# Two GNN layers on one core: the bf16 split of Q and R moves from the node stage into the first layer's loop over edges

## What is computed

```
h   = relu(layernorm(x))
# layer 0, for every edge (src, dst) with its 64 attributes e
a   = relu([h[src], h[dst], e] @ We1 + be1)        # 320 -> 32
m   = relu(a @ We2 + be2)                          # 32 -> 128
b   = relu([h[dst], m] @ Wn1 + bn1)                # 256 -> 64
n   = relu(b @ Wn2 + bn2)                          # 64 -> 128
x   = x + h + segment_sum(n, dst)
# layer 1
h   = relu(layernorm(x))
msg = ((h @ W[etype])[src] + b[etype]) * weight
x   = x + relu(segment_sum(msg, dst))
```

## Time and profile before

| what | value |
|---|---|
| median of 3 runs | 8001.07 us (7994.84 to 8001.35) |
| the profiled execution, its own time | 7997.6 us |
| its span, first to last instruction | 7995.8 us |
| TensorE busy | 6820.1 us (85%) |
| POOL busy | 5906.7 us (74%) |
| VectorE busy | 4067.4 us (51%) |
| ScalarE busy | 2015.2 us (25%) |
| granted TensorE clock, mean | 0.933 |
| data moved by DMA | 572.29 MB, mean 72 GB/s |

### The profile page before, as it was taken

One profiled execution on the slowest core, in us unless ns is written; L12 is line 12 of the kernel. 1 busy time (PEld: TensorE's weight loads), 2 busy tenths in 40 slices (PEclk: granted clock), 3 DMA queues, 4 the chain that ended last, 5 costly groups with the idle time before them and its releaser, 6 DMA issues.

```text
span 7995.8 us, 199814 instructions
## 1 busy us (share of the span) xinstructions
PE 6820.1 (85%) x52954; PEld 5270.5 (66%) x52954; DVE 4067.4 (51%) x13463; ACT 2015.2 (25%) x4976; POOL 5906.7 (74%) x6251
## 2 busy tenths in 40 slices
PE   5999999999999999999978788888788778878887
PEld 4766666666666666667656666666666666666666
DVE  6444444444444444444455555555555555555555
ACT  5433333333333333333330000000000000000000
POOL 4777777777777777777757777777777777777776
PEclk7999999999999999999988988888888988898888
DMA  6333333333333333333332222222222222222222
GB/s 131 85 83 83 83 83 83 83 83 83 83 83 83 83 83 83 83 83 83 83 85 55 55 55 55 55 55 55 55 55 55 55 55 55 55 55 55 55 55 77
DMA packets 646407, 572.29 MB, mean 72 GB/s; under 512 B 325139, under 2 KB 520987, under 8 KB 645452
## 3 DMA queue, kind: packets, MB, share of 16 engines
q0 software_dynamic: 198624, 253.43, 15.0%
q1 hardware_dynamic: 447324, 313.26, 13.8%
HBM read 544.44 MB, written 21.68 MB: 71 GB/s over the span
## 4 chain that ended last, share of the span: by engine, by line
POOL 43%; issue 26%; PE 20%; DMA 7%; SPq 1%; DVE 1%; POOLq 1%; ACT 1%; DVEq 0%; ACTq 0%
POOL shared L589 30%; POOL rows_place L589 12%; PE bank L1165 12%; DMA rows_place<-h_tab,idx 6%; PE bank L1178 3%; PE bank L1167 2%; SPq L520 1%; ACT h_place L636 1%; PE bank L1180 1%; DMA h_place<-h_tab 0%; PE bank L1076 0%; POOLq L387 0%; POOLq L584 0%; PE bank L1095 0%; DMA qr_tab<-late 0%
## 5 line engine op out<-in xcount | busy, mean ns | idle before, releaser
L589 POOL DMA_INDIRECT shared<-p_tab,idx x3128 | 2956.6, 945 | 994.5 <-issue 957.4
L589 POOL DMA_INDIRECT rows_place<-h_tab,idx x3079 | 2906.4, 944 | 960.6 <-issue 865.6
L1165 PE MATMUL bank<-shared,rows_place 128*128 128x256 f32 x6158 | 1831.9, 449 | 642.5 <-DMA rows_place<-h_tab,idx 387.2
L1165 PEld LDWEIGHTS bank<-shared,rows_place 128*128 128x128 f32 x6158 | 1291.6, 220 | 909.4 <-DMA rows_place<-h_tab,idx 430.2
L982 DVE SCALAR_TENSOR_TENSOR shared<-bank,key,late 128x256 f32<-128x256 f32 x3128 | 1292.6, 476 | 839.7 <-PE bank L1167 687.3
L745 ACT ACTIVATE h_place<-bank 128x256 f32<-128x256 f32 x782 | 300.4, 384 | 3501.8 <-PE bank L1167 2956.8
L1076 PE MATMUL bank<-h_sb,w_tile 128*128 128x128 f32 x6256 | 907.7, 288 | 69.3 <-DVE h_sb L899 0.9
L1076 PEld LDWEIGHTS bank<-h_sb,w_tile 128*128 128x128 f32 x6256 | 758.5, 191 | 279.4 <-DVE h_sb L899 279.0
L899 DVE TENSOR_SCALAR h_sb<-bank,be_col 128x128 f32<-128x128 f32 x782 | 273.9, 350 | 1237.0 <-PE bank L1069 1237.0
L1095 PE MATMUL bank<-wn_half,h_sb 128*128 128x128 f32 x6256 | 890.0, 285 | 0.0
L1178 PE MATMUL bank<-h_place,w_rel_sb 128*128 128x64 f32 x6256 | 852.1, 294 | 0.0
(11 more groups left out here) (98 smaller groups left out, 5081.8 us busy)
## 6 DMA issues: line engine op xcount, KB each, us to landing
rows_place<-in_dst_c SPq DMA_DIRECT2D x782, 192.0 KB
h_place<-h_tab SPq DMA_DIRECT2D x6272, 0.5 KB
shared<-in_edge_cols SPq DMA_DIRECT2D x782, 128.0 KB
shared<-p_tab,idx POOLq DMA_INDIRECT x3128
rows_place<-h_tab,idx POOLq DMA_INDIRECT x3079
qr_w<-qr_tab SPq DMA_DIRECT2D x782, 18.0 KB
qr_tab<-late SPq DMA_DIRECT2D x21, 336.0 KB, 5.5
res<-in_x SPq DMA_DIRECT2D x14, 448.0 KB, 6.9
```

Of the source, the lines that this page charges most:

```text
L589: pool.indirect_dma_start(out=rows_of[s][:, t, :], out_offset=None, in_=table, in_offset=bass.IndirectOffsetOnAxis(ap=idx[k][:, s * TC + t ...
L1165: pe.matmul(bank[s][:, 0:RW], there, hot_rel[s % 2][:, t, :], start=(t == 0), stop=(t == TC - 1))
```

## The change

- The table of Q and R is one f32 table of 96 columns. It is stored group by group in the node stage beside P, from four small buffers `pqr` (two in `late`, two in `rows_place`), which no longer lie in `agg`. The split into parts is gone, and so is its wait. ScalarE copies `pqr` out of PSUM in place of VectorE, and waits before the fifth and each later group until the stores from that buffer have landed.
- In layer 0's loop SP loads the window of 32 f32 rows three times over, into 96 partitions (`qr_f`). For each chunk ScalarE copies 64 of these to PSUM and rounds all 96 to bf16 (`split_first`), VectorE subtracts (`remainder`), ScalarE rounds 64 partitions (`split_second`), and VectorE writes the last 32 (`last_part`). The split of a chunk is spread over the steps two and one ahead of its use (three for `split_first`).
- In the node stage VectorE normalises all 7 tiles (`scale_x`) and POOL takes the relu. Between the layers ScalarE normalises tiles 0 to 3 of a group and POOL tiles 4 to 6, then the relu of those.
- `agg` is cleared at the start, half by POOL and half by ScalarE. `dst_f` is converted in the node stage. The edge types are converted ahead of the work between the layers, not behind it.
- The source indices of the first two quads of chunks are both loaded ahead of the loop.

The core of the diff:

```diff
-    qr_tab = nc.dram_tensor("qr_tab", [3, NPAD, QR], bf16).ap()
+    qr_tab = nc.dram_tensor("qr_tab", [NPAD, QR], f32).ap()
...
+        pqr = [t[:, k * TPG * P:(k + 1) * TPG * P].rearrange("p (j d) -> p j d", d=P)
+               for t in (pqr_late, rows_place) for k in range(2)]
+        qr_f = [hT[0][0:3 * W, s * QR:(s + 1) * QR] for s in range(SL)]
+        ps_split = [bank[7][0:2 * W, s * QR:(s + 1) * QR] for s in range(SL)]
...
# sync, node stage
             for g in range(NG):
                 sp.wait_ge(pqr_copied, 2 * g + 2)
-                sp.dma_start(node_rows(p_tab, g), group(pqr, g)[:, :, 0:H1]).then_inc(p_stored, 16)
-                if g == RANGE_AT:
+                sp.dma_start(node_rows(p_tab, g), pqr[g % PQ][:, :, 0:H1]).then_inc(p_stored[g % PQ], 16)
+                sp.dma_start(node_rows(qr_tab, g), pqr[g % PQ][:, :, H1:P]).then_inc(p_stored[g % PQ], 16)
+                if g == RANGE_AT - 2:
                     sp.wait_ge(range_set, 3)
...
-            for q in range(NPART):
-                sp.wait_ge(lo_done, q + 1)
-                for t in range(3):
-                    sp.dma_start(node_rows(qr_tab[t], q * (PT // TPG), PT // TPG), qr_part[q % PB][t]).then_inc(parts_stored[q % PB], 16)
...
# sync, layer 0's loop
-                    sp.wait_ge(h2_summed[s], c.turn + 1)
+                    sp.wait_ge(split_hi[s], c.turn + 1)
                     hold(sp)
-                    sp.dma_start(qr_w[s][:, :], qr_tab[:, ds(start, W), :]).then_inc(qr_landed[s], 16)
+                    sp.dma_start(qr_f[s][:, :], qr_tab[ds(start, W), :].rearrange("(a w) o -> a w o", a=1).broadcast_to([3, W, QR]))\
+                      .then_inc(qr_landed[s], 16)
...
# gpsimd, node stage
+            pool.memset(agg[:, 0:NPAD // 2], 0.0).then_inc(agg_zeroed, 1)
             for g in range(NG):
-                pool.wait_ge(h_done, g + 1)
+                pool.wait_ge(xn_done, g + 1)
+                pool.tensor_scalar_max(h[g % HB], h[g % HB], 0.0).then_inc(relu_done, 1)
+                pool.wait_ge(relu_done, g + 1)
                 pool.tensor_tensor(group(res, g), h[g % HB], group(res, g), ALU.add).then_inc(res_done, 1)
...
# gpsimd, between the layers, behind the memset of a group
+                for j in range(t0, t1):
+                    at = g * TPG + j
+                    ins = pool.tensor_scalar(h[g % HB][:, j, :], res[:, at, :], mv[:, at, 0:1], rstd[:, at:at + 1],
+                                             ALU.subtract, ALU.mult)
+                ins.then_inc(h_high_scaled, 1)
+                pool.wait_ge(h_high_scaled, g + 1)
+                pool.tensor_scalar_max(h[g % HB][:, t0:t1, :], h[g % HB][:, t0:t1, :], 0.0).then_inc(h_high_done, 1)
...
# scalar, layer 0's loop
+            def split_first(c):
+                s = c.slot
+                act.wait_ge(qr_landed[s], 16 * c.turn + 16)
+                act.activation(ps_split[s], qr_f[s][0:2 * W, :], ACT.Copy)
+                act.activation(qr_w[s][:, :], qr_f[s][:, :], ACT.Copy).then_inc(split_hi[s], 1)
+
+            def split_second(c):
+                act.wait_ge(split_res, c.n + 1)
+                act.activation(qr_w[c.slot][0:2 * W, :], ps_split[c.slot], ACT.Copy).then_inc(split_mid, 1)
...
# vector, node stage
+            def scale_x(g):
+                if g >= HB:
+                    dve.wait_ge(h_transposed, 2 * (g - HB + 1))
+                    dve.wait_ge(res_done, g - HB + 1)
+                for j in range(TPG):
+                    at = g * TPG + j
+                    ins = dve.tensor_scalar(h[g % HB][:, j, :], res[:, at, :], mv[:, at, 0:1], rstd[:, at:at + 1],
+                                            ALU.subtract, ALU.mult)
+                ins.then_inc(xn_done, 1)
...
# vector, layer 0's loop
+            def remainder(c, before=None):
+                s = c.slot
+                dve.wait_ge(split_hi[s], c.turn + 2)
+                if before:
+                    last_part(before)
+                dve.tensor_tensor(ps_split[s], ps_split[s], qr_w[s][0:2 * W, :], ALU.subtract).then_inc(split_res, 1)
+
+            def last_part(c):
+                s = c.slot
+                dve.wait_ge(split_mid, c.n + 1)
+                dve.tensor_tensor(qr_w[s][0:W, :], ps_split[s][0:W, :], qr_w[s][0:W, :], ALU.subtract).then_inc(split_lo[s], 1)
...
# tensor, layer 0's loop
-                pe.wait_ge(qr_landed[s], 16 * c.turn + 16)
+                pe.wait_ge(split_lo[s], c.turn + 1)
```

More of the change, by code:

```diff
@@ L124, in gnn_two_layers @@
         range_row = late[0:1, QC * CH:QC * CH + NROW]
-        pqr = agg[:, :].rearrange("p (j d) -> p j d", d=P)
-        PT = 2 * TPG
-        NPART = NTILE // PT
-        PART = PT * QR // 2
-        PB = 3
-        assert 3 * PB * PART <= 2 * NCH * TC
-        qr_part = [[late[:, (3 * k + t) * PART:(3 * k + t + 1) * PART].bitcast(bf16).rearrange("p (j d) -> p j d", d=QR)
-                    for t in range(3)] for k in range(PB)]
+        PQ = 4
+        assert QC * CH + NROW + 2 * TPG * P <= 2 * NCH * TC and 2 * TPG * P <= SL * TC * D
+        pqr_late = late[:, QC * CH + NROW:QC * CH + NROW + 2 * TPG * P]
         HB = 4
@@ L463, in layer0_pass, with step @@
                 hold(sp)
-                def step(c, k, two):
+                def step(c, k, later):
                     s = c.slot
@@ L485, in layer0_pass @@
                 load_idx(0, 0, idx_landed)
-            parts_all_stored(sp)
+                load_idx(1, 1, idx_landed)
+            tables_stored(sp)
             with sp.Fori(0, passes) as m:
                 layer0_pass(m)
-            sp.wait_ge(idx_landed[0], passes * (16 * NQ // 2) + 16)
-            hold(sp)
+            for k in range(2):
+                sp.wait_ge(idx_landed[k], passes * (16 * NQ // 2) + 16)
+                hold(sp)
             load_idx(0, 0, idx1_landed)
@@ L630, in std_of, with normalise @@
                    .then_inc(std_done, 1)
-            def normalise(n, g):
-                act.wait_ge(shift_done, n + 1)
-                for j in range(TPG):
+            def normalise(g):
+                act.wait_ge(shift_done, g + 1)
+                for j in range(*HALVES[0]):
                     at = g * TPG + j
@@ L645, in copy_hT, with copy_pqr @@
                        .then_inc(hT_copied, 1)
+            def copy_pqr(g):
+                if g >= PQ:
+                    act.wait_ge(p_stored[g % PQ], 32 * (g // PQ))
+                for a, (t0, t1) in enumerate(HALVES):
+                    act.wait_ge(pqr_ready, 2 * g + a + 1)
+                    act.activation(pqr[g % PQ][:, t0:t1, :], tiles_of(banks_of(2 * g + 1, 4)[a], t1 - t0), ACT.Copy)\
+                       .then_inc(pqr_copied, 1)
             act.wait_ge(zeroed, 5)
-            for g in range(NG + 2):
+            act.activation(agg[:, NPAD // 2:], zero_col[:, :].broadcast_to([P, NPAD // 2]), ACT.Copy).then_inc(agg_zeroed, 1)
@@ L649, in _ @@
+            for g in range(NG + 3):
                 if g < NG:
                     std_of(g, g)
[L651 to L657 removed]
+                if 2 <= g <= NG + 1:
+                    copy_hT(g - 2)
+                if g >= 3:
+                    copy_pqr(g - 3)
+                if g == NG:
+                    act.wait_ge(dstf_landed, 16)
+                    act.activation(dst_f[:, :], dst_f[:, :].bitcast(i32), ACT.Copy).then_inc(edges_set, 1)
@@ L703, in _, with step @@
             passes = number_of_passes(act)
-            def step(c, before, before2, after):
+            def step(c, before, before2, after, after2, after3):
                 if before:
@@ L822, in count_passes @@
                 dve.tensor_scalar_add(passes_i[:, :], range_i[:, 1:2], 1).then_inc(passes_set, 1)
-            for g in range(NG + 3):
+            for g in range(NG + 1):
                 if g < NG:
@@ L909, in bias_msg2, with step @@
                 dve.tensor_tensor(msg2_sb[:, :], ps_msg2[:, :], bn2_rep[:, :], ALU.add).then_inc(msg2_biased, 1)
-            def step(c, before, before2, after):
+            def step(c, before, before2, after, after2, after3):
                 if c:
                     relu_h1(c)
+                if after2:
+                    remainder(after2, after)
+                elif after:
+                    last_part(after)
                 if after:
```

140 lines of the change are left out of this document (65 added, 75 removed).

## The result

The changed kernel takes 8018.35 us (median of 14 runs, 8017.19 to 8020.19), the kernel before beside it 8000.75 us (14 runs, 7994.84 to 8002.68). The ratio is 1.0023, with a 95% interval from 1.0015 to 1.0031. **It is 18 us slower where I had forecast 48 us less**; the point, the range and the sign were wrong.

The account below looks back on a forecast made before the run. POOL's gathers, 1.249 us each, were taken to pace both loops. 7997.6 less 41.5 (node stage) and 5.5 (between layers) gave 7950.6 us, 7952 as median; range 7934 to 7975, faster 0.88.

Parts of the forecast that it names:

- T, the first gather: End of the node stage: layer 0's first gather at 92 us against 133.5 counted back, a gain of 41.5 us.
- The relu has no row ... I take it near the first, 0.9: Node stage: POOL's relu put near the clearing's 0.84 us, at 0.9, within 4.2 us per group.
- the inserted reductions and the like: Node stage: two range reductions add 7.0 us; pass count, first windows and ramps add 2.8.
- the stores not the estimated 6: Node stage: new waits of 2 us for the first stores and 4 for the ranges' trip through memory.
- A scaling on VectorE: Node stage: each of VectorE's seven scalings per group taken as 0.15 us, 1.1 us for seven.
- The lock itself: Node stage: VectorE's scalings wait until POOL's running operation ends; without that wait T comes 10 us earlier.
- Layer 0's loop: Added ScalarE copies, 0.8 us per chunk, and VectorE subtractions, 0.5, fill idle time: cost 0, gathers still 1.249 us.
- on TensorE's ring: Layer 0's loop: the split's added work delays TensorE; half exposed, 235 us on, 8138; chance 0.05.
- on POOL standing for VectorE: Layer 0's loop: new VectorE operations hold up gathers, 0.25 us per chunk, 195 us on, 8146; chance 0.02.
- Between the layers: ScalarE relieved, POOL's 2.6 us per group below VectorE's 2.98: gain 5.5 us, ends 0 and 7.
- the conversion of the edge types is hidden: Between the layers: the 2.83 us conversion, moved in front, hides behind layer 0's last chunks; uncovered, up to 3 us.
- Layer 1's loop: The second loop follows POOL at an unchanged 1.249 us per gather, so earlier gains move it whole.

Follow-up runs that it names:

- experiment 1: Changed kernel with ScalarE normalising all seven tiles between the layers and POOL only clearing there: 7971.29 us against 7996.64 for the kernel before, ratio 0.9966.

## Why the prediction was wrong

The profiled execution ended 8018.1 - 7950.6 = 67.5 us behind the forecast. By its steps:

- **T, the first gather: 92 forecast, 107.7 measured, 15.7 us.** The term that failed is "The relu has no row ... I take it near the first, 0.9". It measured 2.45. The group's period came out at 5.81 instead of 4.2, and 13 x 1.61 = 20.9. My upper bound, the addition's 2.09, was too low as well: it took the price of another operation for a ceiling. Other terms went the other way: the inserted reductions and the like 3.0 less, the stores not the estimated 6 (their wait lay behind POOL); behind the last group 2.4 more, 1.1 more ahead of the first. 20.9 - 3.0 - 6 + 2.4 + 1.1 = 15.4.
- **A scaling on VectorE: 0.15 forecast, 0.27 measured.** It did little harm: three of the seven start before POOL's addition or with it, and 1.2 us are exposed where I had 1.1.
- **The lock itself: right.** 3.73 against 1.89 us. The Trainium skill ("SBUF — State Buffer", section "Who interferes with whom") names tensor_scalar in VectorE's two-port modes among what waits for a whole GpSimd instruction, and the trace agrees for the addition. For POOL's relu it is not clear: the first scaling, which starts 0.44 us before the relu's end, takes 521 ns in place of 334.
- **Layer 0's loop: right.** Gathers at 945 ns, TensorE's period at 4.65, copies of 0.23 to 0.27 and subtractions of 0.24 and 0.25 us, no stop of POOL. The loop took 1.8 us more than counted back. Both slower rivals, on TensorE's ring and on POOL standing for VectorE, did not occur. The first of them was also priced wrongly: half exposed it comes to 7950.6 + 235 = 8186, not 8138. And the second of the two subtractions writes `qr_w`, not PSUM, and both read it (L933 and L938), so the premise that they keep to PSUM was wrong; no POOL gather was held up by them all the same.
- **Between the layers: 5.5 us of gain forecast, 17.5 of loss measured, 23.0 us.** The step that failed: "even at the addition's rate of 2.09 / 896 us per column, 1.8 for 3 scalings and their relu: 2.6, below 2.98". It is 2.36 for the scalings, 6.2 ns per column where I had 2.33, and 1.18 for the relu, 3.1 ns per column: 0.84 + 2.36 + 1.18 = 4.4. I called it a bound, but it was the price of another operation. With it, ScalarE's waits for `h_tab` would have followed. That the conversion of the edge types is hidden was right: 2.81 us at 4029.00, and ScalarE waited 0.23 us for TensorE behind it.
- **Layer 1's loop: no change assumed, 25.3 us measured.** The step: "the second loop behind it, which follows POOL". It does follow POOL, but POOL's own pace per gather was taken as fixed, by the earlier trace rows, because it was the same in two loops. It was the same in two loops of one program. Removing POOL's work between the layers gives it back, as experiment 1 shows; what links them is open.
- The tail took 1.7 us more. 15.7 + 1.8 + 23.0 + 25.3 + 1.7 = 67.5.

Had I sized the two POOL terms right, the sum would have been about 7950.6 + 14 x 1.55 + 23.0 = 7995, no change. The sign was then set by the gathers. I gave 0.07 to slower and put all of it on rivals in the loop where the new work is; the loss came from engines that I had made busier elsewhere.

## What to carry to other kernels

An engine's rate for an operation it has no row for is not bounded by its other operations: on POOL a one-input relu cost more per column than a two-input addition, and a scaling with two operands per partition 2.6 times as much, so where a forecast moves work to an engine without a row, the range has to take several times the nearest price. When one engine paces thousands of equal instructions, look first at the duration of that instruction in both kernels: 8 ns on each of 3079 outweighed the 24.1 us that the edit had gained up to the end of layer 0. And a wait that a slow stage hides comes out when the stage is mended, as the first stores did.

## What the runs showed of the hardware

- POOL: relu of 128 x 896 f32 2.45 us and of 128 x 384 1.18; subtract and multiply with two operands per partition, 128 x 128, 0.79 us each; addition of 896 columns 2.10; memset of 896 0.84. VectorE does the relu of 896 in 0.63 and the scaling of 128 in 0.27. The Trainium skill ("GPSIMD Engine Reference", section "Engine selection") says that POOL's one-input work is roughly at line rate and its two-input work about twice as slow as VectorE's; here the one-input relu is 3.9 times as slow as VectorE's, and the measurement decides.
- The first gather behind a POOL scaling takes about 1.04 us in place of 0.95, for one time only.
- The pace of all gathers of a loop can shift from 944 to 952 or 955 ns with one instruction of 0.8 to 1.4 us elsewhere in POOL's program, also in the loop that runs before it: 57 us of 8000. What sets it was not found.
